# Row maxima of two heads at once on two row halves of the array, and q and k placed by direct copies

## What is computed

```python
xn = layernorm(x)                                      # per token
q, k, v    = heads(xn @ Wq + bq), heads(xn @ Wk + bk), heads(xn @ Wv + bv)   # 16 heads of 8
att  = einsum('bhqd,bhkd->bhqk', q, k) * scale;  att = where(causal, att, -inf)
y    = einsum('bhqk,bhkd->bhqd', softmax(att), v)      # "self"
qc, kc, vc = heads(xn @ Wcq + bcq), heads(ctx @ Wck + bck), heads(ctx @ Wcv + bcv)
y   += einsum('bhqk,bhkd->bhqd', softmax(qc kc^T * scale), vc)               # "cross"
x    = x + tanh(g_xattn) * (y @ Wp + bp)
xn2  = layernorm(x); combine = route(xn2)              # 4 of 16 experts, by groups
x    = x + tanh(g_ffn) * sum_e combine[:, e] * ((silu(xn2 @ Wg[e]) * (xn2 @ Wu[e])) @ Wd[e])
```

## Time and profile before

| | us |
|---|---|
| median of three runs | 421.1 (417.36 to 424.77) |
| the profiled execution | 423.1 |
| its span, first to last instruction | 421.4 |
| TensorE / VectorE / ScalarE / GpSimd busy | 371.8 / 271.8 / 211.9 / 178.9 |
| 48 stores of parts, 96 loads of stacks on SP | 128 KB and 192 KB each |

### The profile page before, as it was taken

How to read it: one execution, slowest core, us unless ns; L and a number is a source line. 1 busy time by engine, 2 the same in 40 slices (tenths; PEclk the granted TensorE clock), 3 DMA queues, 4 the chain that set the end, 5 groups by cost and what they waited for, 6 DMA issues and landing times.

```text
span 421.4 us, 8947 instructions
## 1 busy us (share of the span) xinstructions
PE 371.8 (88%) x3200; PEld 261.9 (62%) x3200; DVE 271.8 (64%) x760; ACT 211.9 (50%) x442; POOL 178.9 (42%) x286
## 2 busy tenths in 40 slices
PE   0667899999996999999989979996999999998486
PEld 0433265665763778677757765764976876765464
DVE  2223987767736877787689662785588867238652
ACT  1323016677661846584667444671367558663020
POOL 8545210344442386227624650043720661480605
PEclk9999999999996999999999996998799999999799
DMA  4465455002440554064406440047303200400450
GB/s 132 176 187 181 152 170 179 23 2 64 139 120 2 131 150 139 17 141 148 138 12 153 138 126 3 26 127 142 121 2 63 42 15 6 98 15 5 98 111 18
DMA packets 31325, 39.13 MB, mean 93 GB/s; under 512 B 2832, under 2 KB 28592, under 8 KB 28848
## 3 DMA queue, kind: packets, MB, share of 16 engines
q1 hardware_dynamic: 31280, 38.55, 33.7%
HBM read 30.89 MB, written 7.47 MB: 91 GB/s over the span
## 4 chain that ended last, share of the span: by engine, by line
PE 59%; DMA 19%; SPq 7%; DVE 6%; ACT 3%; issue 3%; POOL 2%; POOLq 0%; ACTq 0%
PE bank L726 10%; PE bank L706 9%; PE bank L803 8%; DMA part_scr<-part 7%; DMA comb<-c_scr 6%; SPq L442 6%; PE bank L693 5%; PE bank L794 4%; PE bank L690 4%; PE bank L795 4%; DMA ctx_in<-in_ctxT 3%; PE bank L684 3%; PE bank L745 2%; PE bank L764 2%; DMA c_scr<-combT 2%
## 5 line engine op out<-in xcount | busy, mean ns | idle before, releaser
L848 DVE TENSOR_REDUCE row_max<-bank 128x2 f32<-128x512 f32 (+1 forms) x224 | 148.7, 686 | 69.7 <-PE bank L693 40.6
L618 ACT ACTIVATE probs<-bank 128x512 f32<-128x512 f32 x224 | 128.1, 596 | 71.2 <-PE bank L706 67.4
L706 PE MATMUL bank<-q_stack,k_stack 73*128 73x256 bf16 (+1 forms) x512 | 83.9, 267 | 4.9 <-DMA q_stack<-shiftT 3.2
L726 PE MATMUL bank<-probs,v_ext 128*32 128x256 f32 (+1 forms) x1024 | 64.1, 370 | 0.5 <-ACT probs L618 0.5
L548 POOL TENSOR_TENSOR f_h<-f_h,comb 128x256 f32<-128x256 f32 x64 | 44.6, 725 | 43.1 <-DMA comb<-c_scr 43.1
L534 POOL TENSOR_SCALAR_AFFINE_SELECT probs<-probs 128x256 f32<-128x256 f32 (+1 forms) x96 | 45.2, 483 | 40.2 <-ACT probs L618 39.5
L693 PE MATMUL bank<-k_stack,q_stack 72*128 72x256 bf16 x256 | 53.3, 302 | 3.4 <-DVE row_max L848 2.9
L706 PEld LDWEIGHTS bank<-q_stack,k_stack 73*128 73x128 bf16 x512 | 42.9, 100 | 20.8 <-ACT probs L618 7.9
L803 PE MATMUL bank<-w_down,f_h 128*128 128x128 f32 x256 | 43.0, 308 | 7.2 <-POOL f_h L548 7.1
L794 PE MATMUL bank<-xn2T,w_pairs_sb 128*128 128x256 f32 x128 | 41.0, 402 | 6.4 <-DVE f_h L935 6.3
L726 PEld LDWEIGHTS bank<-probs,v_ext 128*32 128x32 f32 x1024 | 27.5, 111 | 25.3 <-issue 9.8
(11 more groups left out here) (103 smaller groups left out, 435.6 us busy)
## 6 DMA issues: line engine op xcount, KB each, us to landing
q_stack<-part_scr SPq DMA_DIRECT2D x48, 192.0 KB
k_stack<-part_scr SPq DMA_DIRECT2D x48, 192.0 KB
comb<-c_scr SPq DMA_DIRECT2D x16, 512.0 KB, 6.9
part_scr<-part SPq DMA_DIRECT2D x48, 128.0 KB, 2.7
x_in<-in_x SPq DMA_DIRECT2D x8, 128.0 KB, 2.7
w_pairs_sb<-in_w_pairs SPq DMA_DIRECT2D x1, 1024.0 KB, 5.0
out<-y_out SPq DMA_DIRECT2D x8, 128.0 KB, 1.9
ctx_in<-in_ctxT SPq DMA_DIRECT2D x8, 64.0 KB, 2.8
```

The costliest lines, as they stand in the source:

```text
L618: nc.scalar.activation(probs[:, seq % NP, :], exp_bank[s % 2][:, :], ACT.Exp).then_inc(exp_done, 1)
L706: last = pe.matmul(ps[:, n, :], k_stack[0:STACK + 1, b % SLOTS, kind, h, kt * 128:(kt + 1) * 128], q_stack[0:STACK + 1, b % SLOTS, kind, h ...
L726: last = pe.matmul(pv_bank[32 * n:32 * n + VW, col + q0:col + T], v_ext[:, b % 2, kind, kt, 4 * g4 + n, :], p, start=kt == 0, stop=kt == N ...
L848: nc.vector.tensor_reduce(row_max[:, kind, qt, h0:h0 + nh], max_bank[k % 2][:, :].rearrange("p (h k) -> p h k", h=nh), AX.X, ALU.max).then ...
```

## The change

1. *Maxima in pairs.* A max step now covers 1,024 columns, 512 for heads of the lower half (0 to 7) and 512 for heads 8 to 15, in two banks side by side (`max_bank`), which are one buffer. The matmuls use only the first 64 of the 72 rows. Head h works on rows 0 to 63 of the array, head h + 8 on rows 64 to 127, from a second copy (`up`) of the upper heads' stacks that lies in partitions 64 to 127; in batch 0, for which no such copy is made, both work on rows 0 to 63. There are 14 max steps a batch instead of 28, and VectorE takes 1,024 columns with each instruction. The causal matmul comes last, and its two factors are made for 64 rows.
2. *Direct copies.* The scratch tensor is gone. `place_part` copies each part from `part` to the three places where it stands in a stack, 8 rows of 8 KB by each transfer: 36 transfers a batch in place of 18. In batch 0, ScalarE issues those of k. `copy_upper` adds four transfers a batch, from batch 1 on.
3. *Who splits.* Batches 0 and 1 as before; from batch 2 on GpSimd splits both kinds.
4. *Room.* `probs` has 7 buffers instead of 8, f_gate, rest and y_out are gone (their writers work in place), and small tensors share the lower partitions of `upper`.
5. *Order.* All five lists are new.

```diff
-NP = 8
-S1_CHUNKS = [(CROSS, qt, 2 * g, 2, 256) for qt in range(NQ) for g in range(8)]
-S1_CHUNKS += [(SELF, 0, 4 * g, 4, 128) for g in range(4)] + [(SELF, 1, 2 * g, 2, 256) for g in range(8)]
+NP = 7
+S1_CHUNKS = [(CROSS, qt, 2 * g, 2, 256) for qt in range(NQ) for g in range(4)]
+S1_CHUNKS += [(SELF, 0, 4 * g, 4, 128) for g in range(2)] + [(SELF, 1, 2 * g, 2, 256) for g in range(4)]
...
-        rest = sb("rest", [C, 2, 2 * T])
+        upper = sb("upper", [128, 2 * 2 * H2 * T], BF16)
...
-        max_bank, exp_bank, pv_bank, gu_bank, misc = bank[0:2], bank[2:4], bank[4], bank[5:7], bank[7]
+        exp_bank, pv_bank, gu_bank, misc = bank[0:2], bank[2], bank[3:5], bank[5]
+        max_bank = stack.enter_context(nc.psum_tensor("max_bank", [128, 2, 512], FP32))
...
+        def place_part(eng, b, kind, n, qk):
+            eng.wait_ge(split[kind], b * PARTS + n + 1)
+            if n == 0:
+                ge(eng, exp_scores, (b - SLOTS) * NC2 + LAST_OF_KIND2[kind])
+            for m in range(PARTS):
+                row = m * BLOCK + n * D if qk else n * BLOCK + m * D
+                eng.dma_start((q_stack, k_stack)[qk][row:row + D, b % SLOTS, kind].rearrange("d h x -> d (h x)"),
+                              part[:, kind, n, qk * T:(qk + 1) * T]).then_inc(stack_in[b % SLOTS][kind], 16)
...
-            def store_part(b, kind, n):
...
-            def load_stack(b, kind, qk):
...
+            def copy_upper(b, kind):
+                stack_here(sp, b, kind)
+                if b > 1:
+                    sp.wait_ge(max_scores, (b - 1) * NC1 + LAST_OF_KIND1[kind])
+                for qk, st in enumerate((q_stack, k_stack)):
+                    sp.dma_start(up[qk][kind], st[0:HALF, b % SLOTS, kind, H2:H, :]).then_inc(upper_in[kind], 16)
...
+            def max_pair(b, k):
                 kind, qt, h0, nh, keys = S1_CHUNKS[k]
                 if k in (0, CROSS_C1):
                     stack_here(pe, b, kind)
+                    ge(pe, upper_in[kind], 32 * b)
...
-                ge(pe, max_taken, b * NC1 + k - 1)
+                ge(pe, max_taken, b * NC1 + k)
                 s = b % SLOTS
+                ps = [max_bank[:, n, :].rearrange("p (h k) -> p h k", h=nh) for n in range(2)]
                 for n in range(nh):
                     h = h0 + n
+                    for half in range(2):
+                        q, key, at, row = q_stack[0:HALF, s, kind], k_stack[0:HALF, s, kind], half * H2, 0
+                        if half and b > 0:
+                            q, key, at, row = up[0][kind], up[1][kind], 0, HALF
+                        last = pe.matmul(ps[half][:, n, :], q[:, at + h, qt * 128:(qt + 1) * 128], key[:, at + h, 0:keys], start=n == 0,
+                                         stop=kind == CROSS and n == nh - 1, tile_position=(row, 0))
+                if kind == SELF:
+                    for half in range(2):
+                        row = half * HALF if b > 0 else 0
+                        last = pe.matmul(ps[half][:, :, keys - 128:keys], tri_q[row:row + HALF, :], tri_k[row:row + HALF, 0:nh, :],
+                                         start=False, stop=True, tile_position=(row, 0))
                 last.then_inc(max_scores, 1)
```

More of the change, by code:

```diff
@@ L26 @@
 NEG_INF = -1e9
-MASKED = -1e30
 PAD = -3e38
@@ new lines @@
+        exp:5:17 pv:5:3 max:6:7 exp:5:18 y:5 gu:3:2 exp:5:19 exp:5:20 y:5:1 pv:5:4 exp:5:21 exp:5:22 max:6:8 exp:5:23
+        shift:6 exp:5:24 pv:5:5 combT:3 exp:5:25 max:6:9 exp:5:26 wp:4 gu:3:3 pv:5:6 exp:5:27 gu:3:4 max:6:10 y:5:2
+        pv:5:7 gu:3:5 max:6:11 vproj:7 exp:6 gu:3:6 max:6:12 exp:6:1 exp:6:2 y:5:3 gu:3:7 max:6:13 exp:6:3 exp:6:4
+        xn2T:4 exp:6:5 pv:6 exp:6:6 shift:6:1 exp:6:7 down:3 down:3:1 max:7 down:3:2 down:3:3 logits:4 down:3:4
+        max:7:1 exp:6:8 down:3:5 exp:6:9 down:3:6 exp:6:10 down:3:7 gu:4 max:7:2 gu:4:1 exp:6:11 pv:6:1 max:7:3
@@ L270, in build @@
         w_router = w_model_sb[:, 5 * C:5 * C + E]
-        w_ctx_sb = sb("w_ctx_sb", [CC, 2 * C])
+        upper = sb("upper", [128, 2 * 2 * H2 * T], BF16)
+        up = [[upper[HALF:128, (2 * qk + kind) * H2 * T:(2 * qk + kind + 1) * H2 * T].rearrange("p (h x) -> p h x", h=H2)
+               for kind in range(2)] for qk in range(2)]
+        ctx_in = upper[0:CC, 0:2 * NX * T].bitcast(FP32).rearrange("p (n x) -> p n x", n=NX)
+        w_ctx_sb = upper[0:CC, 2 * NX * T:2 * NX * T + 4 * C].bitcast(FP32)
+        low = 2 * NX * T + 4 * C
+        combT = upper[0:E, low:low + 2 * T].bitcast(FP32)
+        shiftT = upper[0:H, low + 2 * T:low + 4 * T].rearrange("p (k x) -> p k x", k=2)
+        ones_row = upper[0:2 * H, low + 4 * T:low + 5 * T]
         w_ck, w_cv = w_ctx_sb[:, 0:C], w_ctx_sb[:, C:2 * C]
@@ L550, in _ @@
             for what, b, n in order("pool"):
-                if what == "vclear":
+                if what == "more":
+                    more_constants()
+                elif what == "vclear":
                     clear_values()
@@ L644, in _ @@
                     first_part(b, n)
+                elif what in ("k0", "k1", "k2"):
+                    place_part(act, b, n, int(what[1]), 1)
                 elif what == "v_e":
```

431 lines of the change are left out of this document (198 added, 233 removed).

## The result

The changed kernel takes **506.9 us** in the median of 4 runs (499.96 to 510.02, of which the profiled one is the longest), against 420.4 for the kernel before in 4 runs beside it (417.4 to 424.8). The ratio is 1.199, 95% interval 1.178 to 1.219: **20% slower**, outside the range of 384 to 450. Of the rivals it is the first, "the target rows pace the copies".

The account below looks back on a forecast made before the run. TensorE (PE) was 88% busy but 59% of the path, transfers with SP's issuing 26%. Start, batch periods and tail gave 236.6 us, 259 copies 168.4: span 405.0, 406.7 with surroundings, forecast median 405 us, range 384 to 450.

Parts of the forecast that it names:

- the target rows pace the copies: Slower rival: eight target rows limit each stack copy, worst case 1.15 us; chance 0.22 above 0.78 us, 0.20 for 0.68 to 0.78.
- p = 0.65: Assumed us per direct stack copy in the queue, between two SBUF-to-SBUF copies and stack loads; 259 copies on the path, 168.4 us.
- four loops: SP's queue paces batches 3 to 6: 9.9 us, 36 copies, 5.6 and 2.7 make 41.6 us each, 166.4 in all.
- The argument against the rival: Neighbouring stack copies go to other rows, so DMA engines that get ahead find them idle.
- 64 KB every 0.65 us never piles up: On the stack-copy queue, earlier waits behind bulk loads (7.5 + 5.7 + 12.5 us) go.
- At most a us or two behind comb's 1 MB: Delay of the shift's landing behind the loads that spread the routing weights, in the loop batches.
- Batch 0: The start: batch 1's first part ends at 29.0, exponentials start at 56.1 us, 4.1 earlier than before.
- The moved waits: nothing, at most 0.6 us each: Given-up buffers and moved waits cost nothing, as other engines finish beforehand; uncovered, each costs at most one exponential's wait.
- TensorE: Paired maxima gain 1.5 us a batch after 0.19 us per group for switching; its own period falls from 40.8 to 39.3.
- The halves don't overlap: Rival: paired max matmuls run one after another, TensorE's period is 43.3 us, total 420; chance 0.12.
- The expected break-even, p = 0.71: Time per stack copy in us at which nothing is won; at 0.75 the kernel is 2% slower.
- Faster: Rival: stack copies issue at the stores' pitch, 0.45 us, then TensorE paces; total 383 us; chance 0.10.

Follow-up runs that it names:

- spread: The changed kernel with each direct copy's 8 target rows lying 8 apart instead of side by side: 452.4 us, 1.081 of the kernel before.
- round 2: Twelve 64 KB copies, each to the next 8 rows, issued behind the changed kernel's last store on an idle chip: 14.2 us, landing 0.97 us each.
- dbl: The changed kernel with stacks filled through DRAM again, and batch 0's max groups alternating between two buffers: 426.4 us, 1.014 of the kernel before.
- spread_all: spread with double max buffer in batch 0, the start order of the kernel before, and shifts ahead of upper copies: 447.6 us, 1.065 of the kernel before.
- direct: The kernel before with stacks filled by direct copies, max still one head at a time: 515.3 us, 1.233 of the kernel before.
- scratch: The changed kernel with its max pairs, but stacks filled through DRAM as before the change: 423.0 us, 1.013 of the kernel before.
- two_q: spread with the 18 k copies of each of batches 3 to 7 issued by ScalarE instead of SP: 450.0 us, 1.077 of the kernel before.
- best: dbl with the earlier start order, shifts ahead of upper copies, and routing-weight transfers ahead of self-stack loads: 412.4 us, 0.989 of the kernel before.

## Why the prediction was wrong, step by step

The sum by its own stages, at p = 0.65, against the traces of the change and of spread, in which a copy costs just that:

| stage | forecast | after | spread |
|---|---|---|---|
| first exponentials | 56.1 | 91.7 | 67.0 |
| to batch 1 | 28.6 | 33.8 | 31.1 |
| to batch 2 | 38.8 | 41.6 | 39.4 |
| to batch 6, four loops | 166.4 | 225.3 | 193.2 |
| to batch 7 | 39.3 | 35.6 | 35.6 |
| after the last start | 75.8 | 80.2 | 79.5 |
| span | 405.0 | 508.3 | 445.8 |

- **The step that failed: "I take p = 0.65".** I priced the issue of a copy, and it is right (0.6 to 0.66 wherever the queue isn't full). What decides is when the queue gets the bytes away: 1.18 us a copy into the same 8 rows, 0.97 into changing ones. The rows make the 62.5 us between the two spans, 24.7 of them before batch 0 and 32 in the loops. (The two profiled executions are the longest of one kernel and the shortest of the other; the medians lie 54.5 apart.) The argument against the rival, that engines that get ahead find other rows idle, is what round 2 tests: it turns 1.18 into 0.97, not into 0.65. With it falls "64 KB every 0.65 us never piles up": the shift lands up to 9.3 us after its issue, for which the sum had 2.7. The bound from the earlier trace rows (1.15) was right; the choice between the ends was not. I went by the pitch of issues in the earlier trace rows, though I had no row on 8 target rows.
- **The four loops, 27 us too short without any effect of the rows.** In the spread trace above: 11.6 us from the exponentials to the first copy (I had 9.9), 25.0 for 36 copies and two small issues, 3.9 for the weights' store, the upper copies and comb, and then 7.1 until the shift lets PE go, where I had 2.7 from the earlier trace rows. "At most a us or two behind comb's 1 MB" was 4.4. By the records of landings the upper copies are down at 228.3 and 229.8, comb's two loads at 232.6 and 235.4, the shift at 235.75: it lands right behind comb, whose 1 MB at the 187 GB/s of the earlier trace rows is 5.6 us, an estimate that I could have made. The two long loops, 50.8 and 54.2, have other causes: 9.5 us for the products with comb before the start of batch 3, and for batch 6 a first copy 17.7 us behind the exponentials (294.2 less 276.5), which in the chain stands behind the products with comb and TensorE's projection of batch 7, and 7.2 of waiting for the store of an output, below.
- **Batch 0.** In the change the start is late by 35.6. The first part of batch 1 ends at 37.2, not 29.0. The trace of ACT (start, busy, ...):

```profile
12.72 2.53 ACTq L388 DMA_DIRECT2D k_stack<-part  x3
...
15.91 4.15 ACTq L388 DMA_DIRECT2D k_stack<-part  x6
...
36.58 0.63 ACT L604 ACTIVATE part<-proj 128x512 bf16<-128x512 f32 x1 [8.46 <-DMA q_stack<-part]
```

  Its copies take 2.53 for three and 4.15 for six, not 1.95 and 3.9, and this first part waits for the transfers of the one before (8.46). Then the placement of batch 1 goes at 0.93 and more, and the shift takes 8.5 to land. In spread that first part ends at 30.0, near my 29.0, and the start is still 10.9 late, in SP's queue:

```profile
35.52 6.42 SPq L389 DMA_DIRECT2D k_stack<-part  x3
...
63.58 0.59 SPq L441 DMA_DIRECT2D q_stack<-upper  x1
```

  The first copy of batch 1 goes at 32.8 instead of 29.0, because copies of batch 0 and the two loads of the experts' weights (31.3 to 32.7) stand in front; the 36 copies last 29.3 us instead of 23.4, most of the excess in the three above, while those weights land (40.7 and 44.6); the input loads, a gap and the landing of the shift take 1.2 more. In the kernel before the weights were issued at 8.2; that the new order moves them in between was in none of my terms. The single buffer made the groups 2.35 us apart where I had under 1.9, but the cross maxima end at 53.6 and ScalarE has their shift at 60.0, ahead of SP: it costs the start nothing here, as dbl and spread_all say too.
- **"The moved waits: nothing, at most 0.6 us each" failed once, for 19.5 us.** The output is now stored from `x1`, so DVE's next addition waits for the store, which SP's order puts behind all of stack 7 and its upper copies, at 375.40, and which lands only 9.45 us after that, where the median store takes 2.4:

```profile
375.40 0.64 SPq L456 DMA_DIRECT2D out<-x  x1
```

  In spread the same wait of PE is 7.2 us. I costed it by the work on DVE and didn't ask what stands ahead of the store on SP.
- **TensorE.** The halves overlap, the switch costs 0.09 each way, VectorE's reduction 1.22. To batch 7 it takes 35.6 us instead of 39.3, but 4.4 us more follow the last start, and the two stages together are 115.9 us where I said 115.1. That feed-forward work went to the tail is my reading: with the order of before they are 43.5 and 73.2 in direct.
- **The rivals.** The price list of the first (457 at p = 0.85, 534 at 1.15) holds 507, but not for its reason alone: of the 103 us between the forecast span and the measured one 62.5 are rows and 41 the terms above. "The halves don't overlap" falls: they start together in scratch. The expected break-even, p = 0.71, was too kind: with p = 0.65 the kernel is at 452, since the other terms already cost 8%. "Faster" wanted p = 0.45; in no kernel here do two such copies follow each other in less than 0.63 us, so it was out of reach.

**Open.** Some batches of the change place 36 copies at 0.66 all through (240.7 to 266.1), others at 0.97 on average (18 copies from 194 to 212, 18 from 356 to 373); which order of target rows or other transfer makes the difference wasn't tried. No run keeps a separate output buffer in the changed kernel, and none leaves the experts' weights at the front of SP's queue. What of the 8% that spread still loses is SP's 36 issues wasn't isolated: two_q takes half of them off SP and gains nothing, since ScalarE then carries them. What best owes to its order alone, without the pairs, wasn't run either.
